# First attention: the score products of a turn ahead of its masks, masks for two heads at once, and weighted values that alternate between column strips

## The reference, cut to what matters

```
q, k, v = (proj(wq), proj(wk), proj(wv))
q = _apply_rope(q, sin, cos)
k = _apply_rope(k, sin, cos)
scores = jnp.einsum('bnth,bnsh->bnts', q, k) * (1.0 / math.sqrt(h))
scores = jnp.where(causal, scores, -jnp.inf)
attn = jax.nn.softmax(scores, axis=-1)
out = jnp.einsum('bnts,bnsh->bnth', attn, v)
```

## Time and profile before

| what | value |
|---|---|
| time, median of 3 runs | 1689.52 us (1683.88 to 1691.61) |
| span of the profiled execution | 1693.6 us |
| TensorE busy in the span | 1574.8 us, 93% |
| VectorE, ScalarE, GpSimd busy | 67%, 43%, 25% |
| the first attention, 50 to 457 us | 407 us, TensorE busy 393.4 us |

### The profile page before, as it was taken

One profiled execution on the slowest core, in us unless ns is written; L12 is line 12 of the kernel. 1 busy time (PEld: TensorE's weight loads), 2 busy tenths in 40 slices (PEclk: granted clock), 3 DMA queues, 4 the chain that ended last, 5 costly groups with the idle time before them and its releaser, 6 DMA issues.

```text
span 1693.6 us, 26835 instructions
## 1 busy us (share of the span) xinstructions
PE 1574.8 (93%) x9460; PEld 1309.7 (77%) x9460; DVE 1127.2 (67%) x2171; ACT 735.3 (43%) x1996; POOL 431.8 (25%) x328
## 2 busy tenths in 40 slices
PE   4999999998899997979999999999999999966998
PEld 3777776766577775757888888888888888955887
DVE  7555565656599997454677777777777677765454
ACT  3544454544222222132555555555555555532332
POOL 4000000001122217323332424242424343406000
PEclk9888899999899998959999999999999999987999
DMA  6000001001132300021020201011110102010000
GB/s 186 14 13 1 26 1 35 28 1 38 41 128 90 128 0 19 1 64 38 26 63 26 63 25 51 30 31 39 30 55 25 62 25 62 25 44 19 1 25 25
DMA packets 39683, 67.81 MB, mean 40 GB/s; under 512 B 4941, under 2 KB 13800, under 8 KB 39619
## 3 DMA queue, kind: packets, MB, share of 16 engines
q1 hardware_dynamic: 37522, 65.69, 12.3%
q10 hardware_dynamic: 2096, 1.30, 0.3%
HBM read 60.65 MB, written 2.13 MB: 37 GB/s over the span
## 4 chain that ended last, share of the span: by engine, by line
PE 70%; DVE 17%; issue 7%; POOL 3%; ACT 2%; DMA 1%; SPq 0%; POOLq 0%; DVEq 0%; ACTq 0%
PE PS L325 14%; PE PS L327 14%; PE PS L326 14%; PE PS L1525 5%; PE PS L1481 3%; DVE E_p L1253 3%; PE PS L1506 3%; PE PS L1527 3%; DVE E_nb L1244 2%; DVE E_mx L1240 2%; PE PS L1788 2%; PE PS L1459 2%; PE PS L1492 2%; DVE E_T L1262 1%; PE PS L1484 1%
## 5 line engine op out<-in xcount | busy, mean ns | idle before, releaser
L325 PE MATMUL PS<-XNH,E_WL 128*128 128x256 f32 x768 | 218.8, 285 | 6.7 <-POOL E_WL L440 5.9
L326 PE MATMUL PS<-XNL,E_WH 128*128 128x256 f32 x768 | 215.3, 280 | 0.0
L327 PE MATMUL PS<-XNH,E_WH 128*128 128x256 f32 x768 | 215.0, 280 | 0.0
L526 POOL TENSOR_TENSOR E_sw<-E_sw,rope2s 128x1024 f32<-128x1024 f32 x64 | 103.3, 1615 | 311.6 <-ACT E_sw L578 311.6
L1240 DVE TENSOR_REDUCE E_mx<-PS 128x4 f32<-128x512 f32 x64 | 60.8, 951 | 142.7 <-PE PS L1774 142.7
L325 PEld LDWEIGHTS PS<-XNH,E_WL 128*128 128x128 f32 x768 | 145.5, 189 | 11.1 <-POOL E_WL L440 8.9
L326 PEld LDWEIGHTS PS<-XNL,E_WH 128*128 128x128 f32 x768 | 145.2, 189 | 1.0
L327 PEld LDWEIGHTS PS<-XNH,E_WH 128*128 128x128 f32 x768 | 145.2, 189 | 0.0
L791 ACT ACTIVATE E_p<-PS,E_nb 128x128 f32<-128x128 f32 (+1 forms) x256 | 103.8, 431 | 86.7 <-DVE E_nb L1244 86.7
L578 ACT ACTIVATE E_sw<-PS 64x256 f32<-64x256 f32 (+1 forms) x128 | 89.5, 699 | 106.3 <-PE PS L327 104.8
L440 POOL TENSOR_TENSOR E_WL<-raw,E_WH 128x512 fp32r<-128x512 f32 x80 | 102.7, 1319 | 124.2 <-ACT E_WH L578 124.2
(11 more groups left out here) (266 smaller groups left out, 4602.7 us busy)
## 6 DMA issues: line engine op xcount, KB each, us to landing
raw<-in_w SPq DMA_DIRECT2D x104, 256.0 KB, 2.9
words<-in_words SPq DMA_DIRECT2D x11, 768.0 KB, 4.3
wo<-in_wo SPq DMA_DIRECT2D x32, 256.0 KB, 3.8
zb<-z_scratch SPq DMA_DIRECT2D x11, 384.0 KB, 4.9
scb<-in_scales SPq DMA_DIRECT2D x11, 384.0 KB, 5.5
X<-in_x SPq DMA_DIRECT2D x8, 256.0 KB, 5.1
SGH<-XNH SPq DMA_DIRECT2D x8, 256.0 KB, 2.7
SGL<-XNL SPq DMA_DIRECT2D x8, 256.0 KB, 2.8
```

The source lines that it names most:

```text
L325: nc.tensor.matmul(o, sl, mh, start=first, stop=False)
L326: nc.tensor.matmul(o, sh, ml, start=False, stop=False)
L327: return nc.tensor.matmul(o, sh, mh, start=False, stop=last)
L526: nc.gpsimd.tensor_tensor(E_sw[:, heads, :], E_sw[:, heads, :], rope2s[:, :].unsqueeze(1).broadcast_to([P, heads.stop - heads.start, SEQ]) ...
```

## The change

In a turn, all eight score products come first, and then the masks. The score products of block 0 have 128 moving columns, not 256, since the rest is masked anyway. One mask product serves the two heads that share a bank: its moving operand is `mask_ts` taken twice. So there are 8 score and 4 mask products a turn, where there were 8 and 8. The waits for `a["vcp"]` and `a["x"]`, which stood ahead of block 1, now stand ahead of all scores. In `weighted_values` the loop over the two strips (`n`) is now innermost.

```
                 if g % 2 == 0:
                     after(pe, a["ot"], pairs)
-                for n in range(2):
-                    c = (2 * g + n) % 4
-                    rows32 = slice(32 * c, 32 * c + 32)
-                    for s in range(2):
-                        for e in range(2):
-                            h = order(2 * n + e)
+                for s in range(2):
+                    for e in range(2):
+                        for n in range(2):
+                            c, h = (2 * g + n) % 4, order(2 * n + e)
+                            rows32 = slice(32 * c, 32 * c + 32)
                             stationary = V0[:, s, 2 * g + n, e, :]
...
+            def scores(g):
+
+                for tb in range(2):
+                    for h in range(4):
+                        r, n = rows(g, h)
+                        at, bank = (h // 2) * SEQ, 2 * tb + h % 2
+                        mm(PS[:, bank, at:at + (tb + 1) * P], qT[r, n, tb * P:(tb + 1) * P], kT[r, n, 0:(tb + 1) * P], start=(h < 2), stop=False,
+                           skip_group_check=True)
+                for tb in range(2):
+                    for e in range(2):
+                        seen = PS[:, 2 * tb + e, :].rearrange("p (h s) -> p h s", h=2)[:, :, tb * P:(tb + 1) * P]
+                        last = mm(seen, identb[:, :], mask_ts[:, :].unsqueeze(1).broadcast_to([P, 2, P]), start=False, stop=True,
+                                  skip_group_check=True)
+                    last.then_inc(a["sc"], 1)
...
-                    for tb in range(2):
-                        if tb == 1:
-                            pe.wait_ge(a["vcp"], b * 4 + (2 + sum(g > v for v in (1, 2, 5, 6) if prepared(b, v))))
-                            if later and g in (1, 2):
-                                pe.wait_ge(a["x"], b * 2 + (g - 2))
-                        for h in range(4):
-                            r, n = rows(g, h)
-                            at, bank = (h // 2) * SEQ, 2 * tb + h % 2
-                            mm(PS[:, bank, at:at + SEQ], qT[r, n, tb * P:(tb + 1) * P], kT[r, n, :], start=True, stop=False,
-                               skip_group_check=True)
-                            last = mm(PS[:, bank, at + tb * P:at + (tb + 1) * P], identb[:, :], mask_ts[:, :], start=False, stop=True,
-                                      skip_group_check=True)
-                        last.then_inc(a["sc"], 1)
+                    pe.wait_ge(a["vcp"], b * 4 + (2 + sum(g > v for v in (1, 2, 5, 6) if prepared(b, v))))
+                    if later and g in (1, 2):
+                        pe.wait_ge(a["x"], b * 2 + (g - 2))
+                    scores(g)
```

## The result

The changed kernel takes 1592.31 us in the median of 4 runs (1588.73 to 1596.49), the kernel before 1688.11 us (one run more than in the table ahead). The ratio is 0.9438, 95% interval 0.9415 to 0.9461: 96 us less.

A forecast was written before the change was run, and what follows sets the result against it. TensorE, through a chain of waits with VectorE in each turn, was taken as the bound; 59 us at full clock plus 21 us from the clock gave 80 us less, 1609.5 us in the median, range 1596 to 1646.

The forecast's parts named there:

- The chain: One turn's waits: scores and masks, VectorE, transposes, weighted values; 10.27 us before, a plain turn forecast at 7.9.
- The block of scores and masks: On TensorE, eight scores in a row, one step, then four masks: 1.44 us in place of 3.72.
- S: Time of the score and mask block: 0.65 + 0.31 + 0.48 = 1.44 us, bounds 1.2 to 1.65.
- What reaches the chain: First score to transposes takes S + 3.85 = 5.29 us, not 6.86: 1.57 us less a turn.
- Weighted values: With alternating strips both run together on TensorE: about 1.5 us in place of 2.32, 0.8 less.
- The moved waits: Scores wait for the values' copy, 0.62 us in 16 turns, 10 us; for X, three turns, 2.5 us.
- The sum at full clock: The phase's gain without clock effects: 76 less 10, 2.5 and 5, about 59 us.
- The clock: Slow stretches begin at the sparse score block; three quarters of their 28 us won, 21 us.
- more than forecast: Case with row halves side by side and no slow stretch left: 1594 us, 4% chance.
- rivals with drained tiles: Every change of row half or strip empties the array: about 1760 us, 5%; half this cost, within 0.5%, 3%.
- no gain of strips: Halves of an fp32 product hold up the other strip in the weighted values: 26 us less gain, 1636, 8% chance.
- a worse clock: Each turn's new idle gap brings as many slow stretches again, 28 us lost: 1658 us, 7% chance.

The follow-up runs named there:

- strips alone: Kernel before with only the weighted values' loop changed so that the two strips alternate; 1659.06 us, ratio 0.984.
- The cut block: Changed kernel with block 0's scores and masks ahead of the waits for the values' copy and X, block 1's behind them; 1577.14 us, ratio 0.9335.
- the three orders tried: Score orders by row half: alternating (changed kernel, 1592.31 us), and on that kernel pairs in the same half (1595.99 us) and four in the same half (1594.29 us).

## Why the prediction was right and wrong

**The chain.** Right. The turn was scores, VectorE, transposes, weighted values, and all four were found again in the forecast order. A plain turn went from 10.19 us to between 7.46 and 7.50; 7.9 were forecast.

**The block of scores and masks.** The mechanism was right (row halves side by side, the cost in the changes), the size was off: S was set to 1.44 and measured 1.10. Of its three terms the scores were taken at 0.65, half way between the bounds, and the step to the masks at 0.31; together 0.96; measured are 0.65 for both (207.21 to 207.86). The masks were 0.48 and are 0.45. The bounds, 1.2 to 1.65, left out the measured value too: 0.31 is the distance from a lone score's start to its mask, and behind the last of a row of scores it is 0.21 (207.65 to 207.86), with 0.45 from the first score to the last, near the lower bound of 0.42. Beside that, trimming and merging, which the sum did not price apart, are worth nothing.

The rule of the Trainium skill that tiles work independently (TensorEngine Tiling (Array Packing), Key Properties) gave S = 1.2. The runs agree with it: S is 1.10, and the first products of the two halves start 0.01 us apart.

**What reaches the chain.** Right: S + 3.85 was worked out for the way from the first score to L1459, and 1.08 to the first maximum was measured for "about S". From the first score to L1459 at 212.06 are 4.85 us, S + 3.75.

**Weighted values.** Right: 1.5 forecast, 1.43 measured with strips alone, and 29 us in place of 26. Strict program order (TensorE: Matmul & The Clock Gate, The mechanism, in the Trainium skill) would have given 1.6. For the starts it does not hold between parts of the array: before, 245.76 lay ahead of 245.86, and four instructions of one strip in a row changed nothing.

**The moved waits.** Right but for the count: up to 0.6 us in 14 turns, not 16, and 0.9 in three, 10.4 us, where 12.5 were forecast. The cut block shows what they cost: of the 0.9 us that it won in a turn behind values about 0.6 is this wait and 0.28 the earlier maximum.

**VectorE.** Named as just fitting into a plain turn of 7.9 us; with the turn at 7.5 its list, with its waits for other engines, is the bound. In the last four turns it is busy for 28.17 of 29.40 us, and the 7.3 us forecast for such a turn were right (7.35). What was wrong is the turn of before: 8.5 us at full clock, read from a stretch that isn't the last four turns, where they took 9.4. So 1 us more a turn was won there than the 1.2 forecast.

**The sum at full clock** was too small: 59 us. The phase is 101 us shorter. One of 24 slow stretches is left, so 23 went, 26 us at 1.15, and about 75 remain for the full clock, 16 more than forecast. The step that failed is the score term S, put at 1.44 us and measured at 1.10: it took the row halves as half overlapped, where they overlap fully, and the step to the masks at 0.31, where it is 0.21. These 0.34 us, 0.1 in what follows and 0.07 in the weighted values are 0.5 us a turn. By the table of turns, 0.5 more than forecast came in the 17 turns that wait for values or `X`, but only 0.3 in the nine plain ones, where VectorE's list stops the gain: 12 us. The other 4 are the last four turns. The 101 us of the phase are those of the two profiled executions; the medians are 96 apart, so up to 5 of the 16 may be no more than the spread from one execution to the next.

**The clock.** The direction was right and shown by two runs: 0.90 with the old block and short weighted values, 0.98 with the new block and long ones. I took three quarters of 28 us, 21; about 26 went. The gap of 0.8 us a turn brought no new stretch: the clock is 1.00 in the first 27 turns (51.69 to 307.36). The one slow stretch left begins at 334.5, in the last turns, and in the 3.4 us ahead of it TensorE was busy for 1.17 us only:

```profile
331.10:334.50 3.40, 1.17 (x14) 0.91 (x16) 3.29 (x10) 3.40 (x17) 0.00 (x0) 1.00 0.69 250
```

**The range.** It ended at 1596 on the low side, just above the case "more than forecast" with its 1594, which had 4%. Two uncertain terms, the halves and the clock, were each set between their ends, and both came out at the favourable one. Rows spoke for it: the strips that ran side by side, and slow stretches that began at the score block. The measured time, 1592, is this case: halves side by side and hardly a slow stretch left. The rivals with drained tiles, with no gain of strips and with a worse clock are refuted by the turns and the granted clock.

## What to carry to other kernels

A small product of another shape between products that use half of the array costs far more than its own time: put those of one shape in a row, and the halves overlap by themselves, in the three orders tried, with up to four instructions of one part in a row; with eight (the strips of before) most of the overlap was lost. Where such a row has to wait for something, put what doesn't need it ahead of the wait, up to where the next engine can start: cutting the row there was worth another 15 us although TensorE's block got longer (1.36 us from first score to transposes, with its waits, not 1.10). In turns in which VectorE's list decides, the same cut gained nothing. And a sparse stretch may cost twice, once itself and once by the clock behind it.

## What the runs showed of the hardware

- Products on the two row halves of the array run side by side: eight of 256 columns and the step to the masks within 0.67 us, and the trimmed ones within 0.65 to 0.67 in three different orders. With four instructions of one half or one strip ahead in the list, the first of the other started 0.01 us after the first, past three waiting ones; with eight in a row (the strips of before) the second strip began only with the first one's fifth.
- With masks between pairs of scores, a change of the array's division costs about 0.21 us, the lost overlap of the halves included (2.37 us for the block against 1.10, six changes more); eight masks of 128 columns or four of 256 in a row cost 0.45 us both.
- The granted clock fell to 1.2 GHz in stretches of 3.4 us and more during or right behind a block of alternating scores and masks, 19 times in the phase, while the profile shows TensorE as hardly ever idle (busy for 336.58 of 339.96 us in the first 27 turns, and for 3.40 of 3.40 ahead of the fall at 228.00). It did not fall behind idle gaps of about 0.8 us between dense work (27 turns at 1.00), and fell once where TensorE had been busy for 1.17 of 3.40 us.
- GpSimd's product of 128x256 beside VectorE's four products of 128x256 made those take 1.62 us, not 1.14.
